# Graph attention on one core: six slots of the schedule, earlier sums and unheld gathers for the last two blocks

## What is computed

```python
q, k, v = x @ Wq + bq, x @ Wk + bk, x @ Wv + bv      # 6250 x 8 heads x 16
scores  = sum(q[dst] * k[src], -1) / 4 + edge @ We + be
e       = exp(scores - segment_max(scores, dst)[dst])
probs   = e / (segment_sum(e, dst) + 1e-10)[dst]
agg     = segment_sum(probs * v[src], dst)
out     = layernorm(x + agg @ Wo + bo)
```

## Time and profile before

| | |
|---|---|
| median of 3 runs | 2427.78 us |
| lowest, highest | 2426.92, 2436.58 us |
| span of the profiled execution | 2449.4 us |
| instructions in it | 25,231 |
| mean granted TensorE clock | 0.786 |
| POOL busy | 1496.0 us (61%) |
| TensorE matmuls busy | 1545.6 us (63%) |
| VectorE busy | 1370.8 us (56%) |

### The profile page before, as it was taken

The page is one execution under the profiler, slowest core; times in us unless marked ns, Lnnn a source line. Parts: engine busy times, 40 slices in busy tenths (PEclk is TensorE's granted clock), DMA queues, the critical chain, the costliest instruction groups (busy, mean ns, idle before and its releaser), DMA issues.

```text
span 2449.4 us, 25231 instructions
## 1 busy us (share of the span) xinstructions
PE 1545.6 (63%) x6655; PEld 1051.5 (43%) x6655; DVE 1370.8 (56%) x3214; ACT 454.6 (19%) x1496; POOL 1496.0 (61%) x1572
## 2 busy tenths in 40 slices
PE   5354576657665757566656666566766666666566
PEld 4233454435343434444444444344444444444344
DVE  4254575656555655555655656555555555556556
ACT  1011121212121211111111212111211212111112
POOL 4736546666666666666666666666666666666661
PEclk7677788868778777877887887877878778788878
DMA  6423334343334334343434343434334343434331
GB/s 248 160 84 105 94 101 130 107 123 115 118 117 130 109 108 130 107 131 108 129 108 128 111 129 108 128 108 125 112 113 127 110 128 111 126 111 127 108 106 31
DMA packets 115143, 288.11 MB, mean 118 GB/s; under 512 B 45909, under 2 KB 53856, under 8 KB 107960
## 3 DMA queue, kind: packets, MB, share of 16 engines
q0 software_dynamic: 74624, 203.26, 28.3%
q1 hardware_dynamic: 37628, 76.52, 9.4%
q10 hardware_dynamic: 2748, 6.69, 0.7%
HBM read 274.69 MB, written 11.67 MB: 117 GB/s over the span
## 4 chain that ended last, share of the span: by engine, by line
PE 40%; issue 25%; another core or an unknown queue 14%; DVE 10%; POOL 9%; DMA 1%; ACT 1%; DVEq 0%; ACTq 0%; POOLq 0%
PE ps_q L1230 14%; PE ps_a L1266 11%; POOL kv_buf L523 9%; PE ps_e L1242 2%; PE ps_t L1216 2%; PE ps_t L1210 2%; DVE prod L850 1%; DVE score L860 1%; DMA kv_buf<-kv_table,src_i 1%; PE ps_s L1294 1%; DVE wv L870 1%; PE ps_a L1319 1%; DVE run_fwd L912 1%; PE ps_a L1320 1%
## 5 line engine op out<-in xcount | busy, mean ns | idle before, releaser
L523 POOL DMA_INDIRECT kv_buf<-kv_table,src_i x1536 | 1465.6, 954 | 899.6 <-issue 407.5
L1230 PE MATMUL ps_q<-q_blk,hots 128*128 128x256 f32 x1564 | 566.4, 497 | 553.8 <-issue 553.6
L1230 PEld LDWEIGHTS ps_q<-q_blk,hots 128*128 128x128 f32 x1564 | 351.9, 246 | 677.7 <-issue 625.2
L1266 PE MATMUL ps_a<-wv,hots 128*128 128x272 f32 x1564 | 559.9, 490 | 8.5 <-issue 5.6
L613 ACT ACTIVATE hots<-ps_t 128x512 f32<-128x512 f32 x377 | 225.1, 597 | 1784.8 <-remote 1035.1
L850 DVE TENSOR_TENSOR prod<-ps_q,kv_buf 128x512 f32<-128x512 f32 (+1 forms) x392 | 268.7, 685 | 497.8 <-remote 322.7
L870 DVE TENSOR_TENSOR wv<-kv_buf,ps_w 128x512 f32<-128x512 f32 (+1 forms) x392 | 266.3, 679 | 238.8 <-remote 179.5
L1266 PEld LDWEIGHTS ps_a<-wv,hots 128*128 128x128 f32 x1564 | 335.4, 238 | 61.0 <-issue 10.4
L860 DVE TENSOR_REDUCE score<-prod 128x32 f32<-128x512 f32 (+1 forms) x392 | 267.2, 682 | 7.9 <-issue 0.2
L930 DVE TENSOR_TENSOR_SCAN ps_s<-seq_far,seq_left,ps_s 8x512 f32<-8x512 f32 x57 | 72.7, 1275 | 188.0 <-remote 155.0
L1309 PE MATMUL ps_a<-sums_sb,carry_from 128*1 128x136 f32 x112 | 28.0, 342 | 195.2 <-DVE sums_sb L982 154.8
(11 more groups left out here) (157 smaller groups left out, 1398.1 us busy)
## 6 DMA issues: line engine op xcount, KB each, us to landing
edge_f<-in_edge_blk SPq DMA_DIRECT2D x55, 1024.0 KB
kv_buf<-kv_table,src_i POOLq DMA_INDIRECT x1536
kv_table<-kv_buf ACTq DMA_DIRECT2D x12, 512.0 KB, 3.2
xt_blk<-in_x_t SPq DMA_DIRECT2D x114, 32.0 KB
out<-y_out SPq DMA_DIRECT2D x114, 32.0 KB
kv_buf<-in_x_perm SPq DMA_DIRECT2D x5, 512.0 KB
codes<-code_table SPq DMA_DIRECT2D x108, 10.5 KB
code_table<-kv_buf SPq DMA_DIRECT2D x1, 1344.0 KB
```

Of the source, the lines that this page charges most:

```text
L523: pool.indirect_dma_start(kv_buf[:, b % NBUF, t, :], None, kv_table, bass.IndirectOffsetOnAxis(ap=src_i[:, column:column + 1], axis=0)).th ...
L1230: one = pe.matmul(ps_q[q % 2][:, k * 2 * D:(k + 1) * 2 * D], hots[:, (v - 1) % 2, 0, k * P:(k + 1) * P], q_blk[:, b % QBUF, :], start=True ...
L1266: one = pe.matmul(sums(b), hots[:, (v - 1) % 2, 1, k * P:(k + 1) * P], wv[:, q % 2, 2 * k:2 * k + 2, :].rearrange("p j w -> p (j w)"), sta ...
```

## The change

The slots of a block become a list. Blocks 0 to 54 keep seven. Blocks 55 and 56, which have four steps and three, get six. The first sum of a block is no longer at a fixed distance. It comes five slots after the block's last slot, or when the sums of the block before are over, or five slots after the sums of the block before that one, whichever is last. The nodes of a block follow its own last sum instead of a seventh slot. And the three holds on the gathers no longer apply to blocks 55 and 56, while the wait for the buffer stays.

The slots that follow, before and after:

| | block 54 | block 55 | block 56 |
|---|---|---|---|
| steps spread from | 378, same | 385, same | 392, now 391 |
| chain offset 0 | 385, same | 392, now 391 | 399, now 397 |
| first weighing for the sums | 390, same | 397, same | 404, now 402 |
| nodes from | 397, same | 404, now 401 | 411, now 405 |

The last slot is 413 instead of 419. The number of slots with matrices is 405 both times. No operation is added or removed but for the waits.

```diff
+    SPACE = [SLOT] * (NB - 2) + [max(SLOT - 1, GS[b]) for b in (NB - 2, NB - 1)]
+    START = [sum(SPACE[:b]) for b in range(NB + 1)]
+    SPREAD_AT = [START[b] + g for b, g in STEPS]
+
+    FIRST_SUM = []
+    for b in range(NB):
+        own = START[b + 1] + LAG
+        before = FIRST_SUM[b - 1] + GS[b - 1] if b >= 1 else own
+        bank_free = FIRST_SUM[b - 2] + GS[b - 2] + LAG if b >= 2 else own
+        FIRST_SUM.append(max(own, before, bank_free))
+    SUM_AT = [FIRST_SUM[b] + g for b, g in STEPS]
+    STEP_AT, WEIGH_AT = ({v: q for q, v in enumerate(at)} for at in (SPREAD_AT, SUM_AT))
+    CHAIN_AT = {START[b + 1]: b for b in range(NB)}
+    NODE_AT = {FIRST_SUM[b] + GS[b]: b for b in range(NB)}
...
         def chain(v, offset):
 
-            b, g = divmod(v - SLOT - offset, SLOT)
-            return b if 0 <= b < NB and g == 0 else None
+            return CHAIN_AT.get(v - offset)
 
         def at_node(v, offset):
 
-            return chain(v, LAG + SLOT + offset)
+            return NODE_AT.get(v - offset)
...
-        SLOTS = range(SLOT * (NB + 2) + LAG + 9)
+        SLOTS = range(max(NODE_AT) + 9)
 
         def hots_in(v):
 
-            return step_in(v + 1), step_in(v - SLOT - LAG)
+            return step_in(v + 1), weighed_in(v)
...
-                        if b >= HELD and t == t0:
+                        if HELD <= b < NB - 2 and t == t0:
                             pool.wait_ge(s_byedge, q - AHEAD + 1)
-                        if b >= HELD and t == t0 + 1:
-                            pool.wait_ge(s_matched, HOTS_TO[slot_of(q - AHEAD)])
+                        if HELD <= b < NB - 2 and t == t0 + 1:
+                            pool.wait_ge(s_matched, HOTS_TO[SPREAD_AT[q - AHEAD]])
-                        if b >= HELD and t == t0 + 2:
+                        if HELD <= b < NB - 2 and t == t0 + 2:
                             pool.wait_ge(s_summed, q - AHEAD - SLOT - LAG)
```

More of the change, by code:

```diff
@@ L350, in step_in, with weighed_in @@
         def step_in(v):
[L352 to L357, removed]
+            return STEP_AT.get(v)
+        def weighed_in(v):
+            return WEIGH_AT.get(v)
         def chain(v, offset):
-            b, g = divmod(v - SLOT - offset, SLOT)
-            return b if 0 <= b < NB and g == 0 else None
+            return CHAIN_AT.get(v - offset)
         def at_node(v, offset):
-            return chain(v, LAG + SLOT + offset)
+            return NODE_AT.get(v - offset)
         def steps_over(b, upto):
             return FIRST[b] + sum(1 for t0, _ in STEP[b] if t0 < upto)
-        SLOTS = range(SLOT * (NB + 2) + LAG + 9)
+        SLOTS = range(max(NODE_AT) + 9)
         def hots_in(v):
-            return step_in(v + 1), step_in(v - SLOT - LAG)
+            return step_in(v + 1), weighed_in(v)
         HOT_SLOTS = [v for v in range(-1, SLOTS[-1]) if hots_in(v) != (None, None)]
@@ L381, in steps_to, with sums_to @@
         def steps_to(v):
-            return sum(1 for b in range(NB) for g in range(GS[b]) if b * SLOT + g <= v)
+            return sum(1 for at in SPREAD_AT if at <= v)
+        def sums_to(v):
+            return sum(1 for at in SUM_AT if at <= v)
         def after(engine, name, semaphore, value):
@@ L418, in load_codes @@
                 if b >= CBUF:
-                    last = (b - CBUF) * SLOT + GS[b - CBUF] - 1
-                    sync.wait_ge(s_matched, HOTS_TO[last + SLOT + LAG])
+                    sync.wait_ge(s_matched, HOTS_TO[SUM_AT[FIRST[b - CBUF + 1] - 1]])
                 n = HALF[b] * P
@@ L607, in copy_hots @@
                     act.wait_ge(s_byedge, steps_to(v - 1))
-                if steps_to(v - 2 - SLOT - LAG) >= 1:
-                    act.wait_ge(s_summed, steps_to(v - 2 - SLOT - LAG))
+                if sums_to(v - 2) >= 1:
+                    act.wait_ge(s_summed, sums_to(v - 2))
                 sizes = [0 if q is None else (STEP[STEPS[q][0]][STEPS[q][1]][1] - STEP[STEPS[q][0]][STEPS[q][1]][0]) * W
@@ L692, in _ @@
                         copy_projected(at_node(v, 5))
-                    if step_in(v - SLOT - LAG) is not None:
-                        copy_weights(step_in(v - SLOT - LAG))
+                    if weighed_in(v) is not None:
+                        copy_weights(weighed_in(v))
                     if chain(v, -4) is not None:
@@ L1015, in _ @@
                         runs_of_dst(chain(v, -2))
-                    if step_in(v - SLOT - LAG) is not None:
-                        weigh(step_in(v - SLOT - LAG))
+                    if weighed_in(v) is not None:
+                        weigh(weighed_in(v))
                     if step_in(v) is not None:
@@ L1254, in sum_step @@
             def sum_step(v):
-                q = step_in(v - 1 - SLOT - LAG)
+                q = weighed_in(v - 1)
                 b, g = STEPS[q]
@@ L1341, in _ @@
                         match(v)
-                    if step_in(v - 1 - SLOT - LAG) is not None:
+                    if weighed_in(v - 1) is not None:
                         sum_step(v)
```

## The result

The change makes the kernel slower: 2459.88 us (median of 6 runs, 2447.86 to 2471.39) beside 2429.62 for the kernel before (6 runs), a ratio of 1.0112 with a 95% interval of 1.0081 to 1.0143, or 27 us (the two medians themselves lie 30.3 us apart). That is more than the 16.8 us forecast.

What follows compares the result with a forecast made beforehand. The prediction took POOL's gather issuing and its stops to bound the kernel until the end, where VectorE is nearly full. Terms 21.3 - 3 - 2 - 1.5 + 2 + 0 = +16.8 gave 2444.6 us, range 2424 to 2459.

Steps and rivals of the forecast that it cites:

- The reading of the limit: POOL's unbroken gathers all but stop TensorE's work or signals; it comes free two to four us after POOL stops.
- the stall: Likeliest case: dropped holds let POOL's gathers hold TensorE up in the last blocks; 2436 to 2458 us, chance 0.62.
- the first rival: Nothing measurable: POOL doesn't hold TensorE up, which is late for its own reason; 2428 us, chance 0.28.
- a term of 0 there: What the skill's page implied for the cost of POOL's unbroken gathers, giving a sum of 2428.3 us; not adopted.
- The row: With block 55's hold gone, 17 more gathers go out before POOL stops, delaying everything from slot 384: +21.3 us (0 to 27.9).
- the high end of the term: Weighing (53, 1) done in time, 4 more unbroken gathers, release 1.6 us longer: 27.9 us instead of 21.3.
- trickling: TensorE gets about a fifth of its work done beside the unbroken gathers: -3 us (0 to -5).
- the second stop: POOL's next stop, near 2379, cost VectorE 4.0 us; with eight gathers left, part is saved: -2 us (0 to -4).
- the late holds: POOL's later stops of 1.33, 2.21 and 3.97 us vanish, so the gathers end earlier: -1.5 us (0 to -2).
- The order of the slots: Six slots fewer save nothing by themselves; moved work lengthens some waits and shortens others: +2 us (-4 to +6).
- The end: Last blocks' finish: block 56's carry gains 1.1 us, its earlier exponentials lose about as much: 0 (-1.5 to +2).
- The faster rival: The end runs at its slots' pace, so six fewer save 6 x 2.8 = 16.6 us: 2411 us, chance 0.10.

Runs made afterwards that it cites:

- e10: Changed kernel without the 26 gathers of blocks 55 and 56, SP copying table rows instead: 2461.71 us, 1.0005 of the kernel before (fourth chip).
- e9: Kernel before, old slot order, only the holds of the last two blocks dropped: 2480.74 us, 1.0088 of the kernel before (fourth chip).
- e8: Changed kernel with the three holds back for the last two blocks: 2444.05 us, 1.0063 of the kernel before (third chip).
- e5: Changed kernel measured again, unedited, beside the kernel before: 2465.26 us, 1.0139 of the kernel before (third chip).
- e12: Changed kernel with holds back and eight slots for block 56, its edge chain in old slots: 2469.18 us, 1.0026 of the kernel before (fourth chip).

## Why the prediction was right or wrong

**The reading of the limit: right, on three of four chips.** POOL's unbroken rows hold TensorE up, and the stop of the hold frees it. e10 (POOL quiet: the stall gone), e9 (only the holds dropped: it is there) and e8 against e5 (holds back: 21 us less) show the direction that the rows before only suggested. On the second chip the first rival is simply true for the holds: 1.0000. The rule of the Trainium skill that PE waits on no one ("SBUF — State Buffer", "Who interferes with whom") is one on the ports of SBUF. On the second chip the trace agrees with it. On the first one TensorE idles 25.11 us inside the row, so the rule gave no ground for a term of 0 there; whether a port is the reason no run shows.

**The row: its upper end came true.** I took 17 more gathers, ended by the weighing (53, 1). That weighing trickled through at 2346.39, as the high end of the term had it, so the next stop was (53, 2), the row had 30 gathers instead of 26, and the release took 5.2 us and not 2.15. The step that failed is the choice within the bounds: my own credit for a fifth of TensorE's work getting done in the row meant that one more weighing would be in time. The credits for trickling, the second stop and the late holds came to -6.5; 21.3 - 6.5 = 14.8 us stood against about 21: e5 less e8 is 21.2 us between the medians (18.5 by the ratios, 17.5 in the first stretch), e9 less before 21.1, and the first stretch of the changed kernel 20.7 over before. Counted from the start of the row, the weighing (53, 2) came 24.2 us later than before (42.5 against 18.3), and (53, 3) 20 us later. The second stop did go: from (53, 2) to (53, 3) it takes 5.1 us instead of 9.2.

**The order of the slots: mis-sized, and this is the larger error.** I took +2 (-4 to +6). Measured: 12 us on the second chip, 15 on the third. The places were right: the add behind the scans (2.8 us foreseen, 3.5 found). Two things were missing. "VectorE is nearly full here, so its work, not the slots, sets the pace" made me count only what can be saved, and I took the earlier scans of block 56 for a gain, where they displaced a weighing (5.0 us against 1.6); how much of the loss that is, e12 leaves open. And I priced every TensorE wait by its length alone, while behind the wait of 3.53 us the clock fell to 1.2 GHz. The trace of before had it: the four-tile sum was 1.14 us at 2404.57 and 1.82 at 2400.53.

**The end: right.** 0 forecast; the last stretch went from 18.6 to 19.3 us.

**The sum.** 16.8 us forecast; 27 and 34 measured, and the parts alone add to 0.88% + 0.63% = 1.5%, 37 us. 2427.78 x 1.0112 = 2455.0 lies inside the range of 2424 to 2459, though the raw median of 2459.88 is just outside. Slower by over 0.5% had the largest chance, and it came. The faster rival (2.8 us a slot) had no part in it: no kernel that kept the six slots gained on before.

## What to carry to other kernels

A wait that looks like a brake can be what frees another engine: before dropping one, see in the timeline what goes on in its pause, and measure on more than one chip, since here the same edit costs 0 on one and 0.9% on another. Work moved earlier in an in-order queue gains only where the engine had idle time. Where TensorE ends up waiting longer, price its next matmuls at the lower clock as well.

## What was not expected of the hardware

- The same kernel took 2021 us on one chip and 2428 to 2460 on three others. On the fast one, 1536 gathers in one row, 1.25 us apart, didn't hold TensorE up. Why chips differ in this stays open; no run here could tell.
- By the records, on the first chip TensorE's next matmuls came only 25.1 us after its last ones in a row of 30 gathers, with two late releases of VectorE between (2346.39 and 2359.65), and VectorE got the next one 5.2 us after the last gather. ScalarE's copy, which waits for TensorE's semaphores alone, started 25.4 us after the recorded end of the matmuls that it reads.
- The clock after such a rest: 2.04 us for four matmuls that take 1.03 at full clock, at a granted clock of 0.50. The low clock behind (54, 0), 0.50 to 0.73, is another matter: e9 had as long a row, and 1.00 right behind (54, 0).
